# Layer norms without GpSimd: centring and scaling as one VectorE operation for each of 16 tiles

## What is computed

```python
def _ln_t(v, eps=1e-05):
    m = jnp.mean(v, axis=-1, keepdims=True)
    s = jnp.var(v, axis=-1, keepdims=True)
    return (v - m) / jnp.sqrt(s + eps)
...
t = t + _L2_attn_ref(_ln_t(t), ...)     # 8 heads, softmax
t = t + _L2_ffn_ref(_ln_t(t), ...)      # 8 experts, top 2, gelu
t = t + _L3_attn_ref(_ln_t(t), ...)     # Haar/rotary attention
t = t + _L3_ffn_ref(_ln_t(t), ...)      # 16 experts, top 2, silu
```

## Time and profile before

| | us |
|---|---|
| median of 3 runs (449.23 to 450.18) | 449.83 |
| the profiled execution | 450.27 |
| its span, first to last instruction | 448.3 |
| PE busy | 369.8 (83%) |
| DVE busy | 292.5 (65%) |
| ACT busy | 219.0 (49%) |
| POOL busy | 191.2 (43%) |

### The profile page before, as it was taken

How to read it: one execution, slowest core, us unless ns; L and a number is a source line. 1 busy time by engine, 2 the same in 40 slices (tenths; PEclk the granted TensorE clock), 3 DMA queues, 4 the chain that set the end, 5 groups by cost and what they waited for, 6 DMA issues and landing times.

```text
span 448.3 us, 6934 instructions
## 1 busy us (share of the span) xinstructions
PE 369.8 (83%) x2147; PEld 237.7 (53%) x2147; DVE 292.5 (65%) x691; ACT 219.0 (49%) x545; POOL 191.2 (43%) x186
## 2 busy tenths in 40 slices
PE   4577279999999999997394999763476899999996
PEld 1462166777777777775271344532264355555552
DVE  2857967777787777774962565998994144444443
ACT  1434267777777777784341455532145233434332
POOL 4300035544555455452850000050100888888885
PEclk9867559999999999999656899867588899999999
DMA  7805000000000000000005980000002855444421
GB/s 230 172 0 189 0 0 2 1 2 2 0 0 0 0 0 0 0 2 1 1 0 174 320 258 4 1 0 2 0 1 76 311 187 188 153 164 155 187 94 48
DMA packets 16698, 32.81 MB, mean 73 GB/s; under 512 B 5728, under 2 KB 9504, under 8 KB 16672
## 3 DMA queue, kind: packets, MB, share of 16 engines
q1 hardware_dynamic: 16672, 32.49, 22.3%
HBM read 31.76 MB, written 0.72 MB: 72 GB/s over the span
## 4 chain that ended last, share of the span: by engine, by line
PE 62%; DVE 21%; ACT 7%; issue 5%; DMA 2%; POOL 1%; POOLq 0%; SPq 0%; DVEq 0%; ACTq 0%
PE ps L999 13%; PE ps L1007 7%; PE ps L843 7%; PE ps L854 6%; PE ps L870 6%; PE ps L958 4%; PE ps L950 3%; DVE xn L1495 2%; ACT va_vb L607 2%; DVE ln L1477 2%; DVE XS L375 2%; PE ps L819 1%; PE ps L820 1%; DVE negmax L1547 1%; PE ps L891 1%
## 5 line engine op out<-in xcount | busy, mean ns | idle before, releaser
L494 POOL TENSOR_TENSOR va_vb<-va_vb,rowinv 128x512 f32<-128x512 f32 x64 | 67.1, 1049 | 74.4 <-DVE rowinv L1554 74.4
L999 PE MATMUL ps<-XS,w3hl 128*128 128x512 f32 x256 | 70.0, 417 | 0.7 <-ACT gT L578 0.7
L721 ACT ACTIVATE wy<-ps 128x512 f32<-128x512 f32 x64 | 38.2, 598 | 63.8 <-PE ps L999 63.8
L999 PEld LDWEIGHTS ps<-XS,w3hl 128*128 128x128 f32 x256 | 47.1, 194 | 34.5 <-DVE hid_more L1639 5.7
L607 ACT ACTIVATE va_vb<-ps,negmax 128x256 f32<-128x256 f32 x128 | 59.5, 472 | 10.7 <-DVE negmax L1547 10.3
L1547 DVE TENSOR_REDUCE negmax<-ps 128x2 f32<-128x512 f32 x64 | 44.1, 689 | 10.0 <-PE ps L843 9.0
L843 PE MATMUL ps<-keys_gates,xcur 128*128 128x256 f32 x256 | 48.0, 311 | 2.2 <-DVE keys_gates L1539 2.2
L458 POOL TENSOR_TENSOR xn<-T,lnc 128x512 f32<-128x512 f32 x4 | 4.2, 1042 | 101.3 <-DVE lnc L1485 101.3
L843 PEld LDWEIGHTS ps<-keys_gates,xcur 128*128 128x128 f32 x256 | 35.7, 195 | 14.7 <-issue 8.1
L854 PE MATMUL ps<-consts,va_vb 128*128 128x128 f32 x256 | 40.5, 280 | 2.8 <-POOL va_vb L494 2.4
L870 PE MATMUL ps<-pT,vproj 128*64 128x256 f32 x256 | 34.5, 392 | 0.0
(11 more groups left out here) (305 smaller groups left out, 749.0 us busy)
## 6 DMA issues: line engine op xcount, KB each, us to landing
pT<-gates_row SPq DMA_DIRECT2D x18, 512.0 KB, 4.7
vproj<-gates_row SPq DMA_DIRECT2D x16, 512.0 KB, 4.8
gate_row_keys<-gates_row SPq DMA_DIRECT2D x14, 512.0 KB, 4.7
early<-in_f_in SPq DMA_DIRECT2D x1, 2048.0 KB, 8.9
consts<-in_consts SPq DMA_DIRECT2D x1, 816.0 KB, 5.5
x<-in_x SPq DMA_DIRECT2D x1, 512.0 KB, 3.7
w2raw<-in_f_in SPq DMA_DIRECT2D x1, 512.0 KB, 3.8
out<-in_f_out SPq DMA_DIRECT2D x1, 512.0 KB
```

The lines of the kernel that those rows point to most:

```text
L494: gp.tensor_tensor(prob[:, n % 4], prob[:, n % 4], rowinv[:, n % 4, :].unsqueeze(2).broadcast_to([P, U, N]), ALU.mult).then_inc(S("p_scale ...
L721: act.activation(act_out[:, kk % 2, :], ps[:, 2 * (kk % 3), :], ACT.Silu).then_inc(S("f3_act"), 1)
L999: mm = pe.matmul(ps[:, 2 * (kk % 3) + w, :], w3hl[:, s, e, w * HID:(w + 1) * HID], XS[:, c * CHUNK:(c + 1) * CHUNK], start=(s == 0), stop= ...
```

## The change

GpSimd's part of the norms (`ln_pool`, four instructions in all) goes. VectorE's two ways over the data (subtract: one of 512 columns, GpSimd's other 512; multiply: four of 256) become 16 `tensor_scalar` operations of 64 columns, one for each tile, with the mean and the reciprocal as two per-partition scalars read from `lnc`. The small operation L1487 goes: ScalarE's root takes the variance's sum as it is, scaled by 1/64, and adds the constant as a bias from a new tile, `eps_ln`, which GpSimd fills at the start. The operation that writes the mean (half the sum) is moved behind the one that signals ScalarE, and VectorE waits for its end there.

```diff
+        eps_ln = sb("eps_ln", [P, 1])
...
-        def ln_pool(gp, n):
-
-            gp.wait_ge(S("ln_mean"), n + 1)
-            gp.tensor_tensor(xn[:, 8:16], T[:, 8:16], lnc[:, 1, 8:16].unsqueeze(2).broadcast_to([P, 8, C]),
-                             ALU.subtract).then_inc(S("ln_centred"), 1)
...
+            gp.memset(eps_ln[:], EPS_LN).then_inc(S("eps_ready"), 1)
...
             split_weights(gp, w2hl, w2raw, [slice(0, EXP2)], "w2_loaded", "w2_high", "w2_split")
-            ln_pool(gp, 0)
...
             attention_pool(gp)
-            ln_pool(gp, 1)
             split_weights(gp, w3hl, w3raw, [slice(e, e + 4) for e in range(0, EXP3, 4)], "w3_loaded", "w3_high", "w3_split")
-            ln_pool(gp, 2)
             l3_pool(gp)
-            ln_pool(gp, 3)
...
-            act.activation(lnc[:, 6, :], lnc[:, 5, :], ACT.Sqrt).then_inc(S("ln_std"), 1)
+            act.activation(lnc[:, 6, :], lnc[:, 4, :], ACT.Sqrt, bias=eps_ln[:],
+                           scale=1.0 / C).then_inc(S("ln_std"), 1)
...
-                step(tt(lnc[:, 1, :], me, mo, ALU.subtract))
-                step(tt(lnc[:, 3, :], lnc[:, 1, :], lnc[:, 1, :], ALU.mult))
-                ts(lnc[:, 1, :], lnc[:, 0, :], 0.5, None, ALU.mult).then_inc(S("ln_mean"), 1)
-                step(stt(lnc[:, 4, :], lnc[:, 3, :], C / 4.0, lnc[:, 2, :], ALU.mult, ALU.add))
-                ts(lnc[:, 5, :], lnc[:, 4, :], 1.0 / C, EPS_LN, ALU.mult, ALU.add).then_inc(S("ln_var"), 1)
-                step(tt(xn[:, 0:8], T[:, 0:8], wide(lnc[:, 1, 0:8], t=8), ALU.subtract))
+                step(tt(lnc[:, 5, :], me, mo, ALU.subtract))
+                step(tt(lnc[:, 3, :], lnc[:, 5, :], lnc[:, 5, :], ALU.mult))
+                if n == 0:
+                    dve.wait_ge(S("eps_ready"), 1)
+                stt(lnc[:, 4, :], lnc[:, 3, :], C / 4.0, lnc[:, 2, :], ALU.mult, ALU.add).then_inc(S("ln_var"), 1)
+                step(ts(lnc[:, 1, :], lnc[:, 0, :], 0.5, None, ALU.mult))
                 dve.wait_ge(S("ln_std"), n + 1)
                 step(dve.reciprocal(lnc[:, 7, :], lnc[:, 6, :]))
-                for p in range(4):
-                    q = slice(CT * p, CT * p + CT)
-                    if p == 2:
-                        dve.wait_ge(S("ln_centred"), n + 1)
-                    tt(xn[:, q], xn[:, q], wide(lnc[:, 7, q], t=CT), ALU.mult).then_inc(S("ln_normalised"), 1)
+                for q in range(TILES):
+                    ins = ts(xn[:, q, :], T[:, q, :], lnc[:, 1, q:q + 1], lnc[:, 7, q:q + 1], ALU.subtract, ALU.mult)
+                    if q % CT == CT - 1:
+                        ins.then_inc(S("ln_normalised"), 1)
```

## The result

The changed kernel takes 451.46 us (median of 20 runs, 449.45 to 454.36), the kernel before 449.81 (20 runs beside it, 445.94 to 451.26). The medians lie 1.65 us apart. The ratio of the means is 1.0048, with a 95% interval of 1.0025 to 1.007 (1.1 to 3.1 us): **slower by half a per cent**, in the range of the forecast and on its side.

What follows compares the result with a forecast made beforehand. The norms, chiefly VectorE's work in them, were taken to lie on the path. Norms 0 to 3 add 0.51 + 0.8 + 0.6 + 0.70 = +2.6 us to the median 449.83, giving 452.4, range 449.0 to 454.8.

Steps and rivals of the forecast that it cites:

- The form of the work on the data: The norms' 16 operations of 64 columns with two SBUF scalars: 0.222 us apart, 0.30 for the last, 3.63 us in all.
- The step from one scalar to two: In the 16 operations, the second scalar was taken to add 0.057 us to the distance of 0.165, giving 0.22.
- The rivals that hid one or both scalars: The 16 operations: second scalar hidden, distance 0.165, 449.2 us, chance 0.17; both scalars free, distance 0.10, 445.1 us, chance 0.08.
- the one without overlap: Rival on the 16 operations: 0.34 us each, 5.4 instead of 3.63, kernel 459.5 us; chance 0.05.
- The end of the norm: VectorE's start of L375 in norm 2: 287.82 instead of 287.13, 0.69 us later; norm 3 +0.70, norm 0 +0.51.
- I take its bias and scale at nothing: ScalarE's root in the norm: it still reads 16 numbers, so it was to run from 283.62 to 283.83 as before.
- Downstream: Behind norms 0, 2 and 3: the shift goes through after norms 0 and 3; after norm 2, 0.6 of 0.69 us counts.
- a little slack: Behind norm 2: ScalarE's first evacuation had waited for ScalarE to finish L367, so 0.6 of the 0.69 us was counted.
- worth nothing: Norm 2: TensorE and ScalarE start earlier on the first group of four, without gain, as L375 stands behind all 16.
- something that I don't see: Catch-all case, such as TensorE's clock at another level behind a norm; chance 0.03.
- Norm 1: GpSimd's w3 split ends near 221.8, L375 starts 1.45 us later, L1514 gives back 1.0; TensorE's way sets +0.8 us.
- strict turns: Rival in norm 1: GpSimd and VectorE alternate, the 16 start near 223.0 instead of 221.8, 1.2 us more, 453.6; chance 0.17.

## Why the prediction was right, and where it was not

**The form of the work on the data** was sized well: 16 operations 0.22 us apart, 3.63 us forecast, 3.66 measured. The step from one scalar to two, taken from a duration because no row showed it as a distance, holds (0.163 to 0.224). The rivals that hid one or both scalars are out; so is the one without overlap.

**The end of the norm** was forecast 0.69 us later and came 0.89 later in norms 2 and 3. The term that was too small is "I take its bias and scale at nothing": the bias tile makes the root 0.31 us instead of 0.21. The reciprocal also started 0.10 us after the root's end (281.17 + 0.31 to 281.58), not 0.04; before, VectorE had not been waiting for it. In norm 0 the remainder came 0.74 later against 0.51; there the copy behind it took 0.57 instead of 0.42 as well, and why I don't know. The first key's remainder is 0.90 later.

**Downstream**: norms 0 and 3 pass it on, as forecast (+0.90; +0.91 at the gates' transposes, of which the profiled execution shows 0.62 behind the DMA). Norm 2 was forecast at +0.6, "a little slack", and came at +2.01 in the profile. The mechanism is another, in two ways. That the first group of four is ready earlier was called "worth nothing"; it frees ScalarE earlier, and with TensorE's clock held up the whole 0.89 us are absorbed (-0.13). With the clock low the projections are the bound, the 0.89 goes through, and the order of the rotary products adds to it: +1.8 to +2.1 against the kernel before in three profiles. TensorE's clock stood in the prediction only under "something that I don't see", with 0.03.

**Norm 1** was forecast at +0.8 and came at -0.36 (-0.55 at L797). The mechanism was right in each piece: the split begins at the attention's end, the small operations are held up one by one, L1506 takes 0.29. The size was off because I took the split to end 9.8 us after the norm's first statistic, with 0.8 us of VectorE's operations let in between. It ended 9.07 after (217.29 + 2.34 = 219.63), for the small operations hardly hold GpSimd up. They also did not take strict turns: L1474 went ahead of a cast, and the root began 0.02 us before the last subtraction instead of behind it. So the remainders came 0.44 us later than before, not 1.45, and the 1.0 us of L1506 outweighs that. Of the three small operations that stand behind a semaphore, L1477 and L1480 found GpSimd in possession (2.28 and 0.95 us) and L1474 did not. L1475, which waits for none, was held too (1.03).

The sum, +2.6, stands against +1.65 of the medians (+2.2 by the ratio of the means, interval 1.1 to 3.1). Term by term, forecast and profile: norm 0 +0.51 and +0.90, norm 1 +0.8 and -0.36 (-1.05 up to norm 2), norm 2 +0.6 and +2.01, norm 3 +0.70 and +0.62. Two terms were too small and one had the wrong sign, and they cancel. That it came out right to 0.9 us was in good part luck. The sign was not: with GpSimd's split out of norm 1 and TensorE's clock held behind norm 2 the new form costs 1.9 us.

## What to carry to other kernels

One VectorE operation for each small tile, with scalars from SBUF, costs by its number: at 64 columns 0.22 us each, while two wide passes with a broadcast operand took 2.65 us for what 16 fused ones did in 3.66. "Fused" halves the passes and multiplies the instructions. Before moving work off GpSimd, look which of its operations hold VectorE up: here it was not so much the one that the change removed (about 1 us a norm) as a weight split that could run elsewhere, and moving two splits gained 8.6 us (447.23 to 438.6), more than any form of the norm. Work that comes in pieces can end later and still free the next engine earlier: follow the first piece as well as the last. And when two profiles of one execution each agree in the total, compare them by stage, and look at the spread of the runs, before saying that a change does nothing.

## What the runs showed of the hardware

- A VectorE `tensor_scalar` of 64 columns from SBUF to SBUF, with constants, in a row of 16 starts 0.10 us after the one before it; each scalar read from SBUF adds 0.06 us. A bias read from a tile adds 0.09 us to ScalarE's operation of 16 columns.
- Four VectorE operations in a row with two SBUF inputs, 256 columns each, alternated one by one with GpSimd's casts and subtractions of 1024 columns and took 7.00 us instead of 1.43. Short ones can pass: L1474 did, the next took 1.03 us.
- The granted clock of TensorE fell from 1.00 to 0.50 behind 20 dense matmuls and transposes, with idle time between these (changed kernel) and without (the kernel before with the split held). It stayed at 1.00 with 26 such matmuls and two more behind each group of transposes, and the 32 projections took 3.79 us instead of 6.40 and 6.94.
- A wait that hangs on a DMA's landing decided, from one profiled execution to another, whether VectorE or GpSimd went first at the start: 1.29, 2.13 or 3.85 us for the same two operations.
